# A decoder layer: the opening block's last query heads are placed between the first pair's score steps

## What is computed

```python
x = _layernorm(x + _L0_attn_ref(x, ...))                  # self attention, 4 heads of 64
x = _layernorm(x + _L0_xattn_ref(x, ctx_1024, mask, ...)) # cross attention, 16 heads of 128, 8 for keys
x = _layernorm(x + _L0_ffn_ref(x, ...))                   # 8 experts, 2 for each token, and a shared one
# cross attention
q = (text_hidden @ Wq); k = (vision_tokens @ Wk); v = (vision_tokens @ Wv)
scores = jnp.where(mask, q . k / sqrt(128), -inf); attn = softmax(scores)
out = (attn . v) @ Wo
```

## Time and profile before

| | |
|---|---|
| median of the runs | 1758.07 us |
| the profiled execution's own time, first to last instruction | 1772.4 us |
| PE busy | 1696.6 us (96%) |
| DVE, ACT, POOL busy | 1226.0, 932.4, 662.2 us |
| mean granted clock of PE | 0.985 |
| last query products of phase_a | 191 to 211 us |
| first score product of phase_b | 220.23 us |
| one pair in mid-loop | 82.1 us |

### The profile page before, as it was taken

The page is one execution under the profiler, slowest core; times in us unless marked ns, Lnnn a source line. Parts: engine busy times, 40 slices in busy tenths (PEclk is TensorE's granted clock), DMA queues, the critical chain, the costliest instruction groups (busy, mean ns, idle before and its releaser), DMA issues.

```text
span 1772.4 us, 28874 instructions
## 1 busy us (share of the span) xinstructions
PE 1696.6 (96%) x10034; PEld 1525.3 (86%) x10034; DVE 1226.0 (69%) x3381; ACT 932.4 (53%) x1707; POOL 662.2 (37%) x417
## 2 busy tenths in 40 slices
PE   6999789999999999999999999999999999997986
PEld 6788678999898998989898989899898989887975
DVE  4555367777877768787777777776878787565446
ACT  4433246565656555565656565555556565543532
POOL 1111063333434435343333343443534331435334
PEclk9999999999999999999999999999999999999998
DMA  5133563333232324252333323233424221432322
GB/s 191 52 116 113 179 125 83 44 87 64 62 66 61 67 74 77 60 96 42 86 44 87 66 61 66 62 66 80 75 62 91 42 55 20 99 110 62 114 76 84
DMA packets 103000, 140.36 MB, mean 79 GB/s; under 512 B 37038, under 2 KB 81872, under 8 KB 102736
## 3 DMA queue, kind: packets, MB, share of 16 engines
q1 hardware_dynamic: 60928, 115.53, 27.3%
q10 hardware_dynamic: 38912, 14.80, 4.7%
q0 software_dynamic: 3024, 8.26, 1.7%
HBM read 113.68 MB, written 24.89 MB: 78 GB/s over the span
## 4 chain that ended last, share of the span: by engine, by line
PE 77%; DVE 3%; DMA 3%; issue 2%; ACT 1%; another core or an unknown queue 1%; POOL 0%; ACTq 0%; POOLq 0%; DVEq 0%; SPq 0%
PE b_turn L758 16%; PE b_out L775 9%; PE b_out L777 9%; PE b_out L776 9%; PE b_score L744 8%; PE b_score L746 8%; PE b_score L745 8%; PE b_out L785 5%; PE c_gate L1410 2%; DMA rden_store<-b_rden 2%; PE c_down L1437 1%; PE c_up L1424 0%; DVE c_up L1728 0%; DVE b_p L897 0%
## 5 line engine op out<-in xcount | busy, mean ns | idle before, releaser
L815 ACT CAST b_pT_hi<-b_turn 125x512 fp32r<-125x512 f32 (+1 forms) x768 | 406.3, 530 | 546.2 <-PE b_turn L758 543.8
L911 DVE TENSOR_TENSOR b_pT_lo<-b_turn,b_pT_hi 125x512 fp32r<-125x512 f32 (+1 forms) x768 | 477.8, 623 | 268.4 <-ACT b_pT_hi L815 262.9
L897 DVE CUSTOM_DVE_ANT_0 b_p<-b_score,b_mask_add 128x500 f32<-128x500 f32 x672 | 451.2, 673 | 56.6 <-PE b_turn L758 24.0
L758 PEld LDWEIGHTS b_turn<-ident,b_p 128*125 128x125 f32 x2688 | 409.9, 186 | 57.6 <-issue 1.1
L758 PE MATMUL b_turn<-ident,b_p 128*125 128x128 f32 x2688 | 418.5, 272 | 0.8 <-ACT b_p L821 0.8
L821 ACT ACTIVATE b_p<-b_p,b_shift 128x1500 f32<-128x1500 f32 x224 | 347.4, 1551 | 16.2 <-DVE b_top_min L905 8.3
L775 PE MATMUL b_out<-b_pT_hi,b_c_hi 125*128 125x512 f32 (+1 forms) x768 | 346.8, 452 | 7.2 <-DVE b_pT_lo L911 7.2
L1034 POOL TENSOR_TENSOR b_oT_lo<-b_oT,b_oT_hi 128x896 fp32r<-128x896 f32 x32 | 67.8, 2120 | 622.1 <-ACT b_oT_hi L843 622.1
L776 PE MATMUL b_out<-b_pT_lo,b_c_hi 125*128 125x512 f32 (+1 forms) x768 | 281.2, 366 | 0.0
L777 PE MATMUL b_out<-b_pT_hi,b_c_lo 125*128 125x512 f32 (+1 forms) x768 | 281.2, 366 | 0.0
L744 PE MATMUL b_score<-b_cT_hi,b_q_hi 128*128 128x500 f32 x672 | 264.6, 394 | 9.5 <-DVE b_cT_lo L984 9.5
(11 more groups left out here) (248 smaller groups left out, 2408.8 us busy)
## 6 DMA issues: line engine op xcount, KB each, us to landing
cT_in<-in_ctxT SPq DMA_DIRECT2D x32, 750.0 KB, 11.7
b_c_in<-in_ctx SPq DMA_DIRECT2D x32, 750.0 KB
q_store<-a_fold_in_or_q_stage SPq DMA_DIRECT2D x16, 896.0 KB, 4.0
q_in<-q_store SPq DMA_DIRECT2D x32, 448.0 KB, 8.2
b_rden_all<-rden_store ACTq DMA_DIRECT2D x32, 256.0 KB, 4.4
b_rden_all<-rden_store ACTq DMA_DIRECT2D x32, 192.0 KB, 4.6
b_mask_in<-in_mask SPq DMA_DIRECT2D x32, 187.5 KB, 10.7
slot_store<-c_y2T SPq DMA_DIRECT2D x35, 128.0 KB, 1.7
```

Of the source, the lines that this page charges most:

```text
L758: mm = pe.transpose(turn_bank[n % 3][0:CK, u * 128:(u + 1) * 128], p[slot % 2][:, u, c * CK:(c + 1) * CK], ident[:])
L815: act.copy(pT_hi[:, n % 3, 0:w], turn_bank[n % 3][0:CK, 0:w]).then_inc(hi_done, 1)
L897: dve.tensor_tensor_reduce(out=p[slot % 2][:, u, keys], in0=score_bank[j][:, 0:FW], in1=mask_add[:, b, keys], scale=1.0, scalar=-3.0e38, o ...
L911: dve.tensor_tensor(pT_lo[:, n % 3, 0:w], turn_bank[n % 3][0:CK, 0:w], pT_hi[:, n % 3, 0:w].bitcast(F32), ALU.subtract).then_inc(lo_done, 1)
```

## The change

phase_a no longer has a block of its own: its five engine programs are called at the head of those of phase_b, with no meeting of the engines between. PE computes heads 0 to 2 of the last block ahead of the first pair, heads 3 and 4 behind the fill of step 0 and one head behind each fill of steps 1 to 11; the copies of ACT and DVE stand in the same places. SP loads `q_in` and `cT_in` as soon as block 0 is stored; the four stores of the last queries stand behind the first pair's loads.

Memory that phase_b writes while phase_a still has something in it is guarded tile by tile: ACT's split of `q_in` waits for the last y; POOL's splits for sequence 1 wait for all 16 heads and for the stores of y; the first `weigh` of each of the first two slots waits for the copies from its bank; `load_rden` waits for the stores of y, and the first `scale_out` for the stores of the queries. For this phase_b's tiles are laid out in another order, with `q_hi`, `q_lo`, `cT_hi`, `cT_lo` as one tile for each sequence of a pair, and phase_c's regions follow. `ident` is loaded once. DVE's memsets of phase_b stand behind phase_a.

```diff
-def phase_a(nc, D, semaphore, M_hi, M_lo, q_in, cT_in):
+def phase_a(nc, D, semaphore, M_hi, M_lo, q_in, cT_in, ident, ident_loaded):
...
+        fold_or_stage = sb("a_fold_in_or_q_stage", [128, 2 * XH * F])
         A_hi = sb("A_hi", [128, XH, F], F32R)
         A_lo = sb("A_lo", [128, XH, F], F32R)
-
-        fold_or_stage = sb("a_fold_in_or_q_stage", [128, 2 * XH * F])
+        y = sb("a_y", [PAIR, TILES, F])
+        yT_hi = sb("a_yT_hi", [128, KC, BLK], F32R)
+        yT_lo = sb("a_yT_lo", [128, KC, BLK], F32R)
...
-        block = ctx.enter_context(nc.Block())
-
-        @block.sync
-        def _(sp):
+        def sync(sp):
...
-            store_q(NBLK - 2, range(PARTS))
-
             for part in range(PARTS):
-                sp.wait_ge(q_stored[part], 16 * (NBLK - 1))
+                sp.wait_ge(q_stored[part], 16)
             sp.dma_start(q_in[:], D["q"][:, 0]).then_inc(ahead_loaded, 16)
             sp.dma_start(cT_in[:], D["ctxT"][0]).then_inc(ahead_loaded, 16)
+            store_q(NBLK - 2, range(PARTS))
             store_y(NBLK - 1)
-            store_q(NBLK - 1, range(PARTS))
-            sp.wait_ge(y_stored, 16 * NPAIR)
-            for part in range(PARTS):
-                sp.wait_ge(q_stored[part], 16 * NBLK)
-            sp.wait_ge(ahead_loaded, 32)
+
+            def store_last():
+                store_q(NBLK - 1, range(PARTS))
+                sp.wait_ge(y_stored, 16 * NPAIR)
+                for part in range(PARTS):
+                    sp.wait_ge(q_stored[part], 16 * NBLK)
+
+            return store_last
...
             pe.wait_ge(yT_lo_done, 2 * NBLK)
-            queries(NBLK - 1, range(XH), 2)
+            return lambda *heads: queries(NBLK - 1, heads, 2)
...
-            for h in range(0, XH, 2):
-                take_head(act, act.copy, NBLK - 1, h, 2)
+            return lambda h: take_head(act, act.copy, NBLK - 1, h, 2)
...
-            for h in range(1, XH, 2):
-                take_head(dve, dve.tensor_copy, NBLK - 1, h, 2)
+            return lambda h: take_head(dve, dve.tensor_copy, NBLK - 1, h, 2)
...
+        HEADS_AHEAD = range(3)
+
+        def heads_at(n):
+
+            return [h for h in range(len(HEADS_AHEAD), XH) if max(h - len(HEADS_AHEAD) - 1, 0) == n]
...
+            store_last_opening = opening.sync(sp)
             load_scores(0, 0, first=True)
             load_values(0, 0, first=True)
-            sp.dma_start(ident[:], D["ident"]).then_inc(const_loaded, 16)
             load_q(0, 1)
             load_scores(0, 1, first=True)
             load_values(0, 1, first=True)
+            store_last_opening()
...
-                    if not (first and slot < 2):
+                    if first and slot < 2:
+                        pe.wait_ge(*opening.taken[slot])
+                    else:
                         pe.wait_ge(oT_done, OT_OPS * (SLOTS * i + slot - 1))
...
                 for n in range(STEPS):
                     for slot, m in fills_at(n):
                         fill(i, slot, m, first)
+                    if first:
+                        query_last(*heads_at(n))
                     lag_step(i, n, first)
+
+            query_last = opening.tensor(pe)
+            query_last(*HEADS_AHEAD)
...
+                if i == 0 and slot < 2:
+                    act.wait_ge(*opening.y_stored)
                 act.wait_ge(rden_stored, 16 * (SLOTS * i + slot + 1))
...
                 for n in range(STEPS):
                     lag_step(i, n, first)
                     exp_step(i, n, first)
-            act.copy(q_hi[:, 0, :], q_in[:]).then_inc(q_split, 1)
-            act.copy(cT_hi[:, 0, :], cT_in[:]).then_inc(cT_split, 1)
+                    if first:
+                        for h in heads_at(n):
+                            if h % 2 == 0:
+                                take_last(h)
+
+            take_last = opening.scalar(act)
+            act.wait_ge(*opening.ahead_loaded)
+            act.wait_ge(*opening.y_done)
+            act.copy(q_hi[0][:], q_in[:]).then_inc(q_split, 1)
+            act.copy(cT_hi[0][:], cT_in[:]).then_inc(cT_split, 1)
+            for h in HEADS_AHEAD[0::2]:
+                take_last(h)
...
+                if slot == 0 and first:
+                    for part_stored in opening.stored:
+                        dve.wait_ge(*part_stored)
...
             def pair_dve(i, first=False):
                 for n in range(STEPS):
                     fill_step(i, n, first)
+                    if first:
+                        for h in heads_at(n):
+                            if h % 2:
+                                take_last(h)
                     lag_step(i, n, first)
-
+            take_last = opening.vector(dve)
+            dve.memset(half[:], -0.5).then_inc(const_set, 1)
+            dve.memset(top[:], TOP_MIN).then_inc(const_set, 1)
+            dve.wait_ge(const_set, 2)
...
+            for h in HEADS_AHEAD[1::2]:
+                take_last(h)
...
                     if first:
                         pool.wait_ge(q_split, 2)
                         pool.wait_ge(cT_split, 2)
+                        pool.wait_ge(*opening.queried)
+                        pool.wait_ge(*opening.y_stored)
```

More of the change, by code:

```diff
@@ L575, in _, with phase_b @@
             block_pool(NBLK - 1, last=True)
-def phase_b(nc, D, semaphore, edge, M_hi, M_lo, q_in, cT_in, ident):
+        return Opening(
+            sync, tensor, scalar, vector, gpsimd, ahead_loaded=(ahead_loaded, 32), y_done=(y_done, NPAIR),
+            y_stored=(y_stored, 16 * NPAIR), queried=(q_done, XH * NBLK), taken=[(q_taken[k], QH * NBLK) for k in range(2)],
+            stored=[(q_stored[part], 16 * NBLK) for part in range(PARTS)])
+def phase_b(nc, D, semaphore, edge, opening, M_hi, M_lo, q_in, cT_in, ident, const_loaded):
     with ExitStack() as ctx:
@@ L592, in phase_b @@
         out_bank = [ps(f"out{j}") for j in range(2)]
[L594 to L612, removed]
         oT = sb("oT", [128, XH, 2, S])
@@ L620, in phase_b @@
         mv = sb("mv", [PAIR, 2])
+        sb("spare", [128, 2480])
+        pT_hi = sb("pT_hi", [CK, 3, WIDE], F32R)
+        pT_lo = sb("pT_lo", [CK, 3, WIDE], F32R)
+        p = [None, sb("p1", [128, UNITS[1], CTX])]
+        rden_all = sb("rden_all", [128, 2, WIDE])
+        q_hi, q_lo, cT_hi, cT_lo = [[None, None] for _ in range(4)]
+        for b in (1, 0):
+            q_hi[b] = sb(f"q_hi{b}", [128, ROWS], F32R)
+            q_lo[b] = sb(f"q_lo{b}", [128, ROWS], F32R)
+            cT_hi[b] = sb(f"cT_hi{b}", [128, CTX], F32R)
+            cT_lo[b] = sb(f"cT_lo{b}", [128, CTX], F32R)
+        c_in = sb("c_in", [CK, CH * CD])
+        c_hi = sb("c_hi", [CK, 2, CH * CD], F32R)
+        c_lo = sb("c_lo", [CK, 2, CH * CD], F32R)
+        mask_in = sb("mask_in", [128, CTX], U8)
+        mask_add = sb("mask_add", [128, 2, CTX], BF16)
+        half = sb("half", [PAIR, 1])
+        top = sb("top", [128, 2, UNITS[0], FILLS + 1])
+        top_min = sb("top_min", [128, FILLS + 1])
+        shift = sb("shift", [128, 2, UNITS[0]])
+        den = sb("den", [128, 2, UNITS[0]])
+        rden = sb("rden", [128, 2, UNITS[0]])
+        p[0] = sb("p0", [128, UNITS[0], CTX])
         edge["end"] = nc.sbuf_base
         END = NPAIR - 1
-        const_loaded, const_set = sem("const_loaded"), sem("const_set")
+        const_set = sem("const_set")
         q_loaded, cT_loaded, c_loaded, mask_loaded = sem("q_loaded"), sem("cT_loaded"), sem("c_loaded"), sem("mask_loaded")
@@ L743, in fill @@
                 rows = slice(WIDE * (slot % 2) + 128 * u, WIDE * (slot % 2) + 128 * (u + 1))
[L744 to L746 removed]
+                pe.matmul(out, q_hi[b][:, rows], cT_hi[b][:, keys], start=True, stop=False)
+                pe.matmul(out, q_hi[b][:, rows], cT_lo[b][:, keys], start=False, stop=False)
+                pe.matmul(out, q_lo[b][:, rows], cT_hi[b][:, keys], start=False, stop=True).then_inc(fill_done, 1)
             def turn(i, n, first):
@@ L1023, in scores_in @@
                         pool.wait_ge(cT_split, 2)
-                    split(q_hi, q_lo, q_in[:], q_loaded, n, q_split, fill_done, filled, i, b, first)
-                    split(cT_hi, cT_lo, cT_in[:], cT_loaded, n, cT_split, fill_done, filled, i, b, first)
+                        pool.wait_ge(*opening.queried)
+                        pool.wait_ge(*opening.y_stored)
+                    split(q_hi[b][:], q_lo[b][:], q_in[:], q_loaded, n, q_split, fill_done, filled, i, b, first)
+                    split(cT_hi[b][:], cT_lo[b][:], cT_in[:], cT_loaded, n, cT_split, fill_done, filled, i, b, first)
                 mask_bias(i, b, first)
@@ L1029, in values_in @@
                 n = 2 * i + b
-                split(c_hi, c_lo, c_in[:], c_loaded, n + 1, c_split, pv_done, 2 * CH * (n - 1), i, b, first)
+                split(c_hi[:, b, :], c_lo[:, b, :], c_in[:], c_loaded, n + 1, c_split, pv_done, 2 * CH * (n - 1), i, b, first)
             def oT_rest(i, b):
@@ L1972, in sb @@
```

(1 more changed line is left out.)

53 lines of the change are left out of this document (21 added, 32 removed).

## The result

The changed kernel takes 1747.16 us (median of 4 runs, 1744.03 to 1748.67), the kernel before 1757.97 in runs beside them: ratio 0.9941 [0.9929, 0.9953], 10.8 us faster. Forecast were 14.1 us and 1744.0. The profiled execution spans 1746.0 us. The one shown of before (1772.4) was long behind the last store of the reciprocals: 243.0 us from there to the end, against 227.9 and 228.0 in two later profiles of the same kernel. So spans aren't compared here; pieces between landmarks are.

A forecast was written before the change was run, and what follows sets the result against it. PE was taken to bound the kernel, busy 1696.6 of 1772.4 us. Five pieces gained 19.4 us, less 3.6 idle and 1.7 at half clock: 14.1 us, so 1758.07 becomes 1744.0 us, range 1740 to 1752.

The forecast's parts named there:

- (a): Hand-over between phase_a and phase_b: PE's idle time of 9.47 us goes, as copies, stores and splits lie beside heads.
- (b): PE's first score products behind the hand-over: the half clock there goes, 1.5 us gained.
- (c): PE ahead of the first turn: the 0.76 us wait goes, since heads stand between fills; 0.8 us gained.
- mask wait: New cost at head 5: PE idles 3.6 us (bounds 1.7 and 6) while DVE waits for the mask.
- half clock: New cost behind the idle time at head 5: PE at 0.50 for 3.4 us, 1.7 us lost (bounds 0 and 2.6).
- (d): First pair: PE's 4.97 us idle time goes if slot 0's reciprocals land sooner (bounds 0 and 4.97).
- (e): First pair, behind the 4.97 us idle time: 5.20 us of PE at half clock goes, 2.6 us gained.
- R4: Rival: new tile addresses slow each pair's products by 3 ns, a pair by 1.5 us; 1767 us; 5%.
- the collision: Slot 0's reciprocals' store against the second `c_in`: it would come 3 to 5 us later and meet the queries' last stores.
- The order of the two turns round: First pair: the second `c_in`, issued at 210.4, would precede the store of the reciprocals, issued at 228.6.
- R1: Rival: the reciprocals' store stays late, meeting `c_in` or queries' stores; 6.5 us gained, 1751.6 us; 16%.
- the forecast's own test: Wrong if PE idles over 2 us between first turn and second pair, or a pair takes over 82.5 us.

The follow-up runs named there:

- six_ahead: The changed kernel with six heads instead of three ahead of the first fill; 1749.46 us, 0.9936 of the kernel before.
- all_ahead: The changed kernel with all 16 heads ahead of the first fill; 1747.87 us, 0.993 of the kernel before.
- mask_first: The changed kernel with the first mask issued ahead of the four stores of y; 1746.32 us, 0.9915 of the kernel before.
- both_later: The changed kernel with second and third context loads held until reciprocals' stores land, queries' last stores ahead of the second; 1742.12 us, 0.9926 of before.
- layout_alone: The kernel before with only the new order of tiles and phase_c's regions, no head moved; 1752.49 us, 0.998 of before.
- all_both: The both_later kernel with all 16 heads ahead of the first fill as well; 1739.49 us, 0.9908 of the kernel before.
- before_later: The kernel before with its second context load held until slot 0's reciprocals land; 1753.73 us, 0.9989; on another chip 1754.32 us, 0.996.

## Why the prediction was right, and where not

Means of the three profiles of each kernel, in us:

| piece | forecast gain | measured |
|---|---|---|
| ahead of head 0 | 0 | 192.0 - 192.5 = -0.5 |
| head 0 to first turn: (a), (b), (c), mask wait, half clock | 6.5 | 42.0 - 35.1 = 6.9 |
| first turn to slot 3's store: (d), (e) | 7.6 | 66.7 - 65.2 = 1.5 |
| loop to the last store | 0 (R4: loss) | 1229.0 - 1226.8 = 2.2 |
| behind it (before: two profiles) | 0 | 228.0 - 227.8 = 0.2 |
| sum | 14.1 | 10.3 (the runs: 10.8) |

**(a), (b), (c) held.** No idle time lies between L324 and L753, the splits end in time, and no other idle time but head 5's lies before the first turn. With all heads ahead the wait before the turn is back (0.72 us), as (c) had it.

**The mask wait held**: 3.84, 3.58 and 3.42 us (forecast 3.6), and 1.7 us lost at half clock each time (1.7). Head 5 started 11.5 us behind head 0 (forecast 11.1). That the mask is the cause is shown by six_ahead, all_ahead and mask_first.

**(d) and (e) failed, by the collision's own step.** "The order of the two turns round" put the store of the reciprocals (forecast 228.6, measured 230.22) behind the second `c_in`. It is behind it, even behind its last packet (223.3), and that didn't help. The forecast saw that the store "meets the queries' last stores" and put that meeting at nothing; it gave the reason against itself in the sentence on the queries' stores held up on five engines behind the second `c_in`, and priced that at nothing too, "as SP has slack". The packets show this very thing: from 231.5 on the queries' last stores occupy about five engines, 11/16 of the reciprocals pass at once, and the rest wait. R1 named it in its brackets, at 16%. At 232 only 175 of the queries' packets were left, which five engines would pass in 1.5 us at 0.042 us each (an estimate); they took until 241.1, since they turned slow. So the time lost is made of both: who stood in front on those engines, and the slow stretch, whose cause is open. The 4.97 taken from "the nearest rows are the other 63 stores" was the wrong choice between bounds: those have no queries' stores beside them.

Slot 1's store was in no rival. Its first burst is 275 of 400 packets, 11 times 25, in before and in the changed kernel, so the third `c_in` is in its way in both, issued 7.3 us ahead of it before and 6.7 now. What changed is how long that load takes: its packets were under way for 8.3 us before (255.6 to 263.9) and for 14.0 now (249.8 to 263.8), over a slow stretch. Now SP issues four loads in a row from 242.83, when the queries' stores have landed; whether that is why wasn't tried. both_later gives back 4.8 to 5.1 us between the landmarks, both halves together and in the profile only; how much each of its two waits and the moved stores do wasn't tried.

The Trainium skill ("DMA: Bandwidth & Descriptors", the section on queues, rings and completion order) says that an engine goes round its queues packet by packet; by that rule a slow packet holds up whoever shares its engine. The trace agrees in part. In six_ahead the two queues go nearly one for one (from 235.5 to 238.5, 115 of the reciprocals and 118 of the queries); in the changed kernel none of the 165 passed from 231.6 to 240.1, while some 200 of the queries' packets did, which the rule by itself doesn't give. The page has nothing that makes 896-byte packets take up to 0.9 us.

**R4 fell, with its sign turned.** The tiles' addresses do change the loop, by 0.16 us a pair: faster. layout_alone shows that the new order alone does it. Why is open: PE's busy time has no single group that explains it, and the query products of phase_a went the other way, 0.200 to 0.2025 us from one to the next (0.200 in layout_alone, which leaves phase_a's tiles where they were).

**What would show it**: the first turn at 225 to 228 was 228.16; "ACT's L835 with no wait" was wrong (3.0 us). PE's idle times between turn and second pair were 1.09, 1.51, 0.16 in the first profile, together over 2 us, and 3.99 and 4.37 at one place in the others. By the forecast's own test it failed. The total lies in its range, which takes in part of R1: (d) and (e) gave 1.5 of 7.6 us, and a faster loop, which no rival had and which is luck, gave back 2.2.

**What the interleaving is worth.** Nothing that shows here: with all 16 heads ahead of the first fill the time can't be told from it (1747.87 for 1749.57, intervals overlap). The gain comes from handing memory over without a meeting of the engines, and 2 to 3 us of it from the order of the tiles (2.2 in the loop of the profiles, 3.3 in layout_alone's runs on another chip). The 16.3 us of all_both are made of that, of a first fill behind the last head, where the mask is long ready, and of two waits, and of an earlier issue of the queries' stores, which together keep large transfers away from the small stores.

## What to carry to other kernels

When work is pulled forward, list every transfer that moves with it, and each small store or load whose landing someone awaits; check all of these against all large ones over the next pair, not only the one that collided before, and against what that one holds up in its own queue. Ask when a transfer lands, not when its packets have passed: here the two lay up to 9 us apart. Put a copy that frees a bank ahead of a wait for data that isn't there yet, or run ahead far enough that the data is. Price a stall from more than one profile, and on more than one chip: the same edit gave 2.0 and 7.0 us.

## What the runs showed of the hardware

A store of 512 elements of 4 bytes took 9.5 us from its issue to its landing in before_later and 8.1 in mid-loop (issued at 392.98), with no large transfer beside it and all its packets through in 0.4 us both times. The last store of the changed kernel (384 elements), from the chain that ended last (start, us):

```profile
1519.08 8.06 DMA rden_store<-b_rden
```

Beside a load of the context its packets took 15.9 us in before, beside the queries' stores 10.2 in the changed kernel. Two things add up there. A load of 125 partitions leaves 11/16 of the store alone and holds up the rest, or holds up stores behind it in its queue that then do. And the other transfer's packets turn slow for 7 to 14 us at a time, in every kernel of the study. In the changed kernel POOL splits without a pause from 226.5 to 241.3, and the first such stretch ends with it; the second outlasts POOL's work (257.9) by 5 us. But POOL isn't needed for one: in all_ahead it did nothing from 230.3 to 246.6, and its windows show the stretch all the same:

```profile
231.00:240.00 9.00, 9.00 (x52) 7.72 (x51) 6.49 (x16) 3.93 (x7) 0.00 (x0) 1.00 0.48 26
```

The cause of the slow stretches stays open. The same 487 products of a pair take 81.94 or 82.10 us depending on where the tiles lie. One kernel, before, takes 1755.8 to 1761.6 us on four chips (medians of 11 and more runs on three, one run on the fourth). An idle time of PE of 1.51 us (after) was followed by 3.4 us at clock 0.50; one of 2.19 before wasn't.
